# A recurrent stage on one core: chains folded over three planes by VectorE instead of scanned from an interleaved tile

## What is computed

```
xW = x @ Wx + b
for t in range(128):
    h = tanh(h @ Wh + xW[:, t])
```

## Time and profile before

| what | us |
|---|---|
| median of three runs | 8299.54 |
| first run listed | 8312.09 |
| span of the profiled execution | 8311.2 |
| VectorE busy in the span | 6987.2 (84%) |
| TensorE busy (matmuls) | 6754.2 (81%) |
| ScalarE busy | 4891.1 (59%) |
| GpSimd busy | 1902.8 (23%) |

### The profile page before, as it was taken

One profiled execution on the slowest core, in us unless ns is written; L12 is line 12 of the kernel. 1 busy time (PEld: TensorE's weight loads), 2 busy tenths in 40 slices (PEclk: granted clock), 3 DMA queues, 4 the chain that ended last, 5 costly groups with the idle time before them and its releaser, 6 DMA issues. The chain is left out here.

```text
span 8311.2 us, 122846 instructions
## 1 busy us (share of the span) xinstructions
PE 6754.2 (81%) x38193; PEld 2748.6 (33%) x38193; DVE 6987.2 (84%) x12707; ACT 4891.1 (59%) x5846; POOL 1902.8 (23%) x1514
## 2 busy tenths in 40 slices
PE   4788888888888888888888883588888888782889
PEld 1233333333333333333333331233333333341553
DVE  4799999999999999999999996899999999446333
ACT  3677777777777777777777772244444444222322
POOL 0000001001001001001000110588788888000000
PEclk8999999999999999999999996799999999996999
DMA  1211111111111111111111110000000000000000
GB/s 37 37 27 32 32 27 32 32 27 32 27 32 32 27 32 30 29 32 28 31 32 27 32 32 24 18 4 3 4 3 3 4 3 3 2 6 3 3 15 5
DMA packets 51335, 174.59 MB, mean 21 GB/s; under 512 B 5857, under 2 KB 13794, under 8 KB 49698
## 3 DMA queue, kind: packets, MB, share of 16 engines
q0 software_dynamic: 37264, 145.91, 9.9%
q1 hardware_dynamic: 13586, 22.47, 1.0%
HBM read 15.12 MB, written 7.34 MB: 3 GB/s over the span
## 5 line engine op out<-in xcount | busy, mean ns | idle before, releaser
L980 POOL TENSOR_TENSOR hc<-hh,cg 128x512 f32<-128x512 f32 x1024 | 1290.4, 1267 | 349.8 <-DVE hh L962 349.5
L902 ACT ACTIVATE ps_m<-ps_m,aneg 128x508 f32<-128x508 f32 x1024 | 674.4, 659 | 1121.2 <-DVE hh L962 1011.2
L962 DVE TENSOR_TENSOR_SCAN hh<-ps_m,bx 128x512 f32<-128x512 f32 x1024 | 1228.7, 1213 | 13.7 <-POOL bx L984 13.7
L476 POOL TENSOR_TENSOR r_gate<-ident 128x1 f32<-128x1 f32 x137 | 213.7, 1560 | 4475.4 <-DVE rx_s L564 4413.3
L327 PE MATMUL r_ps<-wdiag,whq 128*128 128x512 bf16 x4480 | 1057.7, 382 | 216.3 <-DVE rh_gain L189 76.4
L866 PE MATMUL ps_m<-hc,pick 128*128 128x512 f32 x2048 | 1056.9, 600 | 8.0 <-POOL hc L980 6.8
L571 DVE TENSOR_TENSOR_SCAN co<-rx_d 128x772 f32<-128x772 f32 x544 | 924.0, 1761 | 0.0
L571 DVE TENSOR_TENSOR_SCAN co<-rh_d 128x772 f32<-128x772 f32 x512 | 862.5, 1747 | 15.6
L300 PE MATMUL r_ps<-rx_nd,ident 128*128 128x512 f32 x1096 | 557.4, 655 | 200.7 <-DMA rx_nd<-rx_s 200.7
L327 PEld LDWEIGHTS r_ps<-wdiag,whq 128*128 128x128 bf16 x4480 | 395.3, 98 | 836.9 <-issue 139.3
L941 DVE TENSOR_TENSOR bx<-ps_m,bg 128x512 f32<-128x512 f32 x896 | 596.8, 672 | 89.4 <-PE ps_m L882 89.0
(11 more groups left out here) (412 smaller groups left out, 11921.0 us busy)
## 6 DMA issues: line engine op xcount, KB each, us to landing
rx_nd<-rx_s POOLq DMA_DIRECT2D x137, 1040.0 KB, 8.0
rows_scratch<-pc SPq DMA_DIRECT2D x48, 128.0 KB
rows<-rows_scratch SPq DMA_DIRECT2D x128, 48.0 KB
ew<-in_e SPq DMA_DIRECT2D x3, 1024.0 KB, 7.4
co<-in_x_dn SPq DMA_DIRECT2D x1, 1024.0 KB, 4.8
xcur<-in_x_dn SPq DMA_DIRECT2D x1, 1024.0 KB
out_x<-xcur SPq DMA_DIRECT2D x1, 1024.0 KB, 3.9
qi<-in_f_q SPq DMA_DIRECT2D x1, 384.0 KB, 3.0
```

The lines of the kernel that those rows point to most:

```text
L902: e.activation(da[un % NDA][:, :, 1:T], ps[:, un % 2, :].rearrange("p (n t) -> p n t", n=NG4)[:, :, 1:T], ACT.Exp, scale=aneg[:, 0:1]).the ...
L962: e.tensor_tensor_scan(hh[un % NBUF][:], da[un % NDA].rearrange("p n t -> p (n t)"), bx[un % NBUF][:], 0.0, ALU.mult, ALU.add).then_inc(sc ...
L980: e.tensor_tensor(hc[un % NHC][:], hh[un % NBUF][:], cg[:], ALU.mult).then_inc(weighted, 1)
```

## The change

- The interleaved tiles are gone. Each side has three planes of 16 x 130 columns: `MINUS_D` (minus the difference), `REM` (the remainder) and `SUM`. The x side has two such sets and alternates between them. A chain is one `tensor_reduce` per four sequences that reads 4 x 128 x 3 numbers, plane innermost, so that consecutive numbers lie 16 x 130 x 4 = 8320 bytes apart, and writes four sums.
- ScalarE no longer copies sums and differences. Of the remainders it makes four plain copies on the h side and one on the x side. The x products are copied once instead of twice.
- The h side goes in two halves of eight sequences: products, sums, difference, residue, remainder, signs. Product and remainder of a half share PSUM banks with the other half's (`PROD`, `REMS`). The matmuls of a half have 256 columns in place of 512, and there are twice as many, but for the first product of each bank, which keeps 512.
- The x difference is two GpSimd `tensor_tensor` instructions of 8 x 128 in place of the DMA, each held until ScalarE has copied a given h remainder. The x bias add moves from VectorE to GpSimd.
- VectorE's order in a step: x scan and x even sums of the first half; scan, even sums and difference of h, half by half; second x scan; two x reduces; two h reduces; two x reduces; x even sums of the second half; two h reduces.
- Dummy matmuls stay at the last two of the seven places; before them TensorE waits until ScalarE has copied the x remainder.

```diff
-        def side(tag):
-            f = dict(pd=sb(tag + "pd", [128, N, K2]), s=sb(tag + "s", [128, N, K2]), d=sb(tag + "d", [128, 2, N * LX + 1]))
...
+        MINUS_D, REM, SUM = 0, 1, 2
+        hz = sb("rh_z", [128, 3, N, K2])
+        hp = sb("rh_p", [128, N, K2])
+        xz = [sb(f"rx_z{i}", [128, 3, N, K2]) for i in range(2)]
+        fold = lambda z, part: z[:, :, part, 2:K2].rearrange("p c n k -> p n k c")
...
-        IN_TANH = ((9, 4), (14, 4), (19, 4), (23, 4), (26, 5), (36, 4), (44, 3))
+        IN_TANH = ((36, 4), (44, 3))
...
+            def h_remainder(c, differenced, seeded, signed):
+                bank0, at = REMS(c)
+                e.wait_ge(*seeded)
+                e.wait_ge(*differenced)
                 for b in range(NB):
+                    e.matmul(ps[:, bank0 + b, half(at)], negid[:], piece(hz, MINUS_D, b, HALVES[c]), start=False, stop=False,
+                             skip_group_check=True)
...
+            def x_remainder(g, i, mov):
+                every = slice(0, N)
+                e.wait_ge(x_summed, 4 * g + 4)
+                for b in range(NB):
+                    e.matmul(ps[:, NB + b, :], negid[:], piece(xz[i], SUM, b, every), start=True, stop=False)
+                e.wait_ge(x_negdiff, 2 * g + 2)
...
-                    h_product(0, KD * t)
-                    stay_warm(4, 5)
-                    residue(0, (ra, KA * t + A_COPIED)).then_inc(rl_mm, 1)
-                    stay_warm(4, 2)
...
+                    h_product(KD * t, ((x_copied, g + 1), (x_rest, g)))
+                    for c in range(2):
+                        residue(c, (ra, KA * t + A_COPIED[c]))
+                    for c in range(2):
+                        h_remainder(c, (v, KV * t + V0 + V_DIFF[c]), (ra, KA * t + A_SEEDED[c]), (ra, KA * t + A_SIGNED[c]))
...
                     for op, count in IN_TANH:
                         e.wait_ge(v, KV * t + V0 + VSUM + op)
-                        stay_warm(1, count)
+                        e.wait_ge(x_rest, g + 1)
+                        stay_warm(NB + 1, count)
...
                     e.activation(t0[:, :, 0], line(xm), ACT.Copy).then_inc(tri, 1)
-                    e.wait_ge(xa, 5 * g + 5)
-                    e.wait_ge(xp_mm, g + 2)
-                    copy_out(X, 4, xa)
-                    copy_negative(xn)
+                    x_rest_copy(g, at)
+                    e.wait_ge(x_folded, NRC * g)
+                    x_copy(g + 1, other)
...
-                e.dma_start(flat(X["nd"][:]), flat(X["s"][:]), accum_op=ALU.add, max_dma_last_dim=4 * N * K2 // 2).then_inc(xd, 16)
...
+            def x_negdifference(g, i, c):
+                e.wait_ge(x_summed, 4 * g + 2 * c + 2)
+                p = xz[i][:, MINUS_D, HALVES[c], 2:K2]
+                e.tensor_tensor(p, p, xz[i][:, SUM, HALVES[c], 2:K2], ALU.subtract).then_inc(x_negdiff, 1)
...
+                    for c in range(2):
+                        e.wait_ge(ra, KA * t + A_REST[2 * c])
+                        x_negdifference(g, (s + 1) % 2, c)
...
+            def x_fold(g, i, lo, hi_):
+                e.wait_ge(x_rest, g + 1)
+                for c in range(lo, hi_):
+                    e.tensor_reduce(xsum[:, i, quarter(c)], fold(xz[i], quarter(c)), mybir.AxisListType.XY, ALU.add).then_inc(x_folded, 1)
...
-                    x_chain(g - 1, s)
-                    e.wait_ge(xc, KXC * g)
+                    x_prefix_odd(g, at, 1)
                     for c in range(NRC):
-                        e.wait_ge(ra, KA * t + A_PUT + 2 * (c + 1))
-                        j = tl.inc(chain(R, quarter(c).start, quarter(c).stop))
+                        if c % 2 == 0:
+                            x_fold(g - 1, s % 2, c, c + 2)
+                        if c == 2:
+                            x_prefix_even(g, at, 1)
+                        e.wait_ge(ra, KA * t + A_REST[c])
+                        j = tl.inc(e.tensor_reduce(ends[:, quarter(c)], fold(hz, quarter(c)), mybir.AxisListType.XY, ALU.add))
```

More of the change, by code:

```diff
@@ L44 @@
 K2 = D + 2
-NP = D // 2
 UN = D // N
@@ L276, in h_product, with piece, residue @@
                         e.wait_ge(diagh, made + (3, 6, 8)[r])
[L277 to L282, removed]
-            def residue(bank0, copied):
+                    for c in range(2):
+                        bank0, at = PROD(c)
+                        if i == 0:
+                            e.wait_ge(*free[c])
+                        for b in range(NB):
+                            if i == 0:
+                                e.matmul(ps[:, bank0 + b, :], h_stat(b, q), diag[rows(b), r].rearrange("p n k -> p (n k)"),
+                                         start=True, stop=False)
+                            else:
+                                ins = e.matmul(ps[:, bank0 + b, half(at)], h_stat(b, q), h_mov(b, r, c), start=False, stop=(i == 5))
+                        if i == 5:
+                            ins.then_inc(rp_mm, 1)
+            def piece(z, plane, b, n):
+                return z[:, plane, n, 2 + KB * b:2 + KB * (b + 1)]
+            def residue(c, copied):
+                bank0, at = PROD(c)
                 e.wait_ge(*copied)
@@ L287, in residue @@
                     for b in range(NB):
-                        ins = e.matmul(ps[:, bank0 + b, :], whn[rows(b), q, :], h_mov(b, r), start=False, stop=(i == 8),
+                        ins = e.matmul(ps[:, bank0 + b, half(at)], whn[rows(b), q, :], h_mov(b, r, c), start=False, stop=(i == 8),
                                        skip_group_check=True)
-                return ins
-            def remainder(bank0, F, stat, mov, prefixed, differenced, diff, last, own=NB, seeded=None):
-                e.wait_ge(*prefixed)
-                for b in range(own):
-                    e.matmul(ps[:, bank0 + b, :], negid[:], piece(F, "s", b), start=True, stop=False)
+                ins.then_inc(rl_mm, 1)
@@ L301, in remainder @@
                 for i, (q, r) in enumerate(LARGE_FIRST):
                     for b in range(NB):
-                        ins = e.matmul(ps[:, bank0 + b, :], stat(b, q), mov(b, r), start=False, stop=(last and i == 8),
-                                       skip_group_check=(b >= own))
-                return ins
-            def sticky(bank0, signed):
+                        e.matmul(ps[:, bank0 + b, half(at)], h_stat(b, q), h_mov(b, r, c), start=False, stop=False, skip_group_check=True)
                 e.wait_ge(*signed)
@@ L309, in sticky @@
                 for b in range(NB):
-                    for c in range(2):
-                        ins = e.matmul(ps[:, bank0 + b, :], tau[:, c, :], R["sg"][:, c, b, :], start=False, stop=(c == 1),
-                                       skip_group_check=(b >= OWN))
+                    for k in range(2):
+                        ins = e.matmul(ps[:, bank0 + b, half(at)], tau[:, k, :], sg[:, k, b, half(c)], start=False, stop=(k == 1),
+                                       skip_group_check=True)
@@ L396, in put_differences @@
[L396 to L409 removed]
+            banked = lambda bank0: ps[:, bank0:bank0 + NB, :].rearrange("p b (n k) -> p n b k", n=N)
```

333 lines of the change are left out of this document (151 added, 182 removed).

## The result

The changed kernel takes 8395.62 us (median of four runs, 8388.67 to 8405.77); beside it the kernel before took 8297.69. The ratio is 1.0116, with an interval of 1.0101 to 1.013: **slower by 1.2%**, where 2.5% faster was forecast. The profiled execution of after took 8405.77 us with a span of 8403.6, 92.4 more than before; the forecast was a span 210 shorter. So 302 us have to be found.

The account below looks back on a forecast made before the run. VectorE, busy 94% of the loop, was taken as the bound. 78 us (its list), 37 (stalls) and 95 (ahead of the loop) made 210 off the 8311.2 span: 8101, as median 8090 us; range 8010 to 9160.

Parts of the forecast that it names:

- The reduce: VectorE's fold of 1536 columns, eight a step: 1.75 us each, 1.67 start to start, as if in order.
- rival A: The fold pays for each hop: eight reduces a step at 2.63 us instead of 1.67, total 9100; chance 0.41.
- a reduce between 1.8 and 2.6: Sign for the fold's measured us: in this range the prediction is wrong in size, at 2.7 in sign.
- If no wait is left before the h scan: Condition on VectorE's 23.42 us list: the h products' copy lands at 2014.54, VectorE is free at 2014.79.
- rival B: In the loop the late x remainder at TensorE's lower clock delays the h product: 1.4 us a step, 8265; chance 0.13.
- The dropped dummy matmuls cost nothing as long as the clock holds: On TensorE, dropping dummies was put at no cost, with the clock's failing left to rival B.
- At no cost: Work on ScalarE, TensorE and GpSimd in the loop was taken as covered by VectorE's reduces, adding nothing.
- The wait of L203 on ScalarE: In 25 loop steps the tanh's scan waits for ScalarE's copies; 37 us less, bounds 0 and 37.
- The rest of VectorE's list: Scans, even sums and differences beside the reduces in a loop step; the whole list 23.42 us against 24.03.
- half-width matmuls: TensorE's h matmuls, twice as many at half the columns, covered by x reduces; 390 us if that cover goes.
- Ahead of the loop: Nine passes before the loop fall from 26.3 to 13.7 us each; 95 us less, bounds 0 and 120.
- rival C: GpSimd's two differences collide with VectorE's scans: 630 us if both stand in front of them, 8720; chance 0.04.

Follow-up runs that it names:

- experiment 10: Changed kernel with all moves of experiment 7 and the plane-by-plane folds of Experiment 9 together: 8093.56 us, ratio 0.9755.
- experiment 7: Changed kernel, second x even sums before all reduces, `xsl` copied between GpSimd's differences, ScalarE's x copies before the tanh's three, dummies at all seven places: 8267.12 us.
- Experiment 9: Changed kernel with one edit, every fold reading plane by plane instead of three planes in turn: 8193.83 us, ratio 0.9872.
- experiment 4: Changed kernel, the four x folds reading plane by plane, two planes in turn, three by pairs, three in turn: 8207.23 us, one run.
- experiment 2: Changed kernel with the `xsl` copy moved between GpSimd's two differences at every eighth step: 8346.1 us, ratio 1.005.
- experiment 1: Changed kernel with the second x even sums moved ahead of all eight reduces: 8395.44 us, ratio 1.0111.
- (6): Changed kernel with the early x even sums of experiment 1 and no dummy matmuls in the tanh: 8429.75 us, ratio 1.015.
- (3): Changed kernel with 30 dummy matmuls on TensorE between the h remainder and the x remainder: 8394.24 us, ratio 1.0108.

## Why the prediction was wrong

The sign was wrong. Three steps failed. As they are priced below, 154 and 107 and 50, they come to 311, 9 more than the 302: of the 107, 27 are waits in the seven back-edge steps, which experiment 10 still has (24), and small terms were not followed up. The runs give the same in another way: experiment 7 takes 128.5 away and the order of reading on top of it (10) another 173.6, together 302.

**The reduce.** The step was "in order the fold is nearest to these multiplies, so I take 1.67". It measured 1.82 to 1.83 from start to start, 14.67 a step instead of 13.47 with the tail: 1.20 x 128 = 154 us, three quarters of the gain forecast. Rows 5 hop over two rows; the change hops over three. The prediction named the number of planes and then used the price of two. Besides, at 32 columns 0.12 ns a number is 4 ns, no more than the two multiplies of rows 5 differ by (192 and 196): they could speak against rival A's 20 ns and not against this. The prediction had itself said that 0.2 us a reduce eats the whole gain and that a reduce between 1.8 and 2.6 would make it wrong in size; with 0.15, together with the other two, it was wrong in sign. Experiment 9 takes this one term back and ends 1.3% below the kernel before.

The Trainium skill ("Vector Engine (DVE) Microarchitecture Reference", section 5.2) gives 1.73 ns a column for a source that hops at each element; by that 1536 would take about 2.7 us (an estimate). The fold at 1.905 us does not bear that out. That page's stream of two regions in turn at full rate agrees with experiment 4 (1024 numbers in 1.235 us), and so does its rule that runs of two neighbours make hops free (1.745 against 1.727). A cycle of three, which it does not name, costs 0.12 ns a number here.

**"If no wait is left before the h scan."** The prediction let the copy land 0.25 us before VectorE needs it. It landed 0.75 late in the common step; the group shows 107.2 us over the loop once the `xsl` steps are set aside (experiment 2). This is rival B's mechanism at about half its price (0.75 for 1.4 a step): the x remainder starts at 2086.43, after 7.50 us of idle TensorE, and its first eight matmuls take 6.60 instead of 3.60. Against B the prediction held that VectorE's 2.1 us of work would cover the copy; it does not. B put the lower clock on the x remainder alone. What neither B nor the forecast had is that its cost falls on whatever TensorE does first after the pause: with the x side early (experiment 1) on the dummies, without dummies on the h product itself (6), and dummies only at one place move the pause (3). "The dropped dummy matmuls cost nothing as long as the clock holds" was the step with the right condition and without a number for it. The wait went only in experiments 7 and 10, where both the order and all dummies were mended.

**"At no cost": GpSimd's queue.** The prediction listed what stands behind the differences, "every eighth step, the operand copies", and went on without asking who waits for these. TensorE's x remainder does: 172.7 us of its idle time before L328 are put down to that copy, 16 times, some 3.3 us later each time than without it. Experiment 2 prices it: 50 us.

**What was right.** The wait of L203 on ScalarE is gone as forecast (37). The rest of VectorE's list was right to 0.06 us a step, the differences on GpSimd take 2.37 in the loop (forecast 2.5 at most), and nothing showed of the half-width matmuls.

**Right in part by luck.** Ahead of the loop 95 us less were forecast and 97 measured. But a pass takes 15.06 (100.06 less 85.00, the first scans of two passes) where 13.7 was worked out, and from the first pass to the ninth 86 us are saved, not 101. The rest comes from a first scan that is 4 us earlier (41.95, before 45.74) and from a stretch between the ninth pass and the first `pre` that is 7.5 us shorter, neither of them in the forecast. The dearer fold lengthens a pass by 0.7 (7.37, worked out as 6.7). What lengthens it most is the mechanism of rival C, which the prediction gave a chance of 0.04 and looked for in the loop alone (columns as in the timelines above):

```profile
87.05 3.22 POOL L475 TENSOR_TENSOR rx_z<-rx_z 128x1024 f32<-128x1024 f32 x1 [3.69 <-DVE rx_z L567]
88.15 2.67 DVE L567 TENSOR_TENSOR rx_z<-rx_z 128x512 f32<-128x512 f32 x1
...
167.15 0.70 DVE L567 TENSOR_TENSOR rx_z<-rx_z 128x512 f32<-128x512 f32 x1
172.56 4.68 POOL L475 TENSOR_TENSOR rx_z<-rx_z 128x1024 f32<-128x1024 f32 x2
```

VectorE's even sums, with two inputs, take 2.67 us beside GpSimd's difference, which itself takes 3.22 instead of 2.36. In the ninth pass, where the differences come later, the same sums take 0.70. Nine of the 18 even sums ahead of the loop are long like this, some 2 us each.

**The rivals.** A had the right term and not its size: 0.12 ns a number more, not 0.625. C fell in the loop, where each difference stands beside reduces, and shows ahead of it, where it stands beside even sums. In the loop step shown, the pair of reduces at 2086.30, with GpSimd's difference beside it, takes 3.72 us, and the pair at 2078.41 without one takes 3.72 too. The Trainium skill ("SBUF — State Buffer", "Who interferes with whom") says the same of `tensor_reduce`, and here the trace agrees.

## What to carry to other kernels

Before a read order that hops is costed, count the regions that it cycles through and look for a row with that count: two in turn were free here, three were not, and a plane-by-plane or pairwise order was. When work is moved to another engine's queue, ask of each instruction already in that queue who waits for it, even if it comes only every eighth step. Where an engine is left idle by design, put a number on its lower clock for the first work after each pause, since taking one late start away can hand the same wait to the next piece of work.

## What was not expected of the hardware

- A one-input reduce over three regions in turn costs 0.12 ns a number more than in order (1.905 us against 1.727 for 1536), at distances of 8320, 8352, 8448 and 16384 bytes alike; two regions in turn, or three by pairs, cost nearly nothing (1.235 us for 1024, 1.745 for 1536).
- A two-input `tensor_tensor` on GpSimd and one on VectorE slow each other down (2.36 to 3.22 us and 0.70 to 2.67, ahead of the loop); beside a reduce both keep their times (2.36 and 3.72 a pair).
- The cost of TensorE's lower clock (granted 0.81 to 0.86 over these loops, 0.50 to 0.55 where it bit) did not go away with the work that bore it. It moved from the x remainder (979 ns a matmul against 592) to the seven dummies (3.15 us against 1.67) and from these to the product itself (614 ns against 380), with 129, 140 and 175 us of wait before the h scan.
